# The causal mask inside the exponents' fp32r product, output rows kept earlier, routing weights later

## The reference, cut to what matters

```python
Lmat = jnp.exp(_segsum(Ac))          # exp(cs[l] - cs[s]) for s <= l, exp(-inf) = 0 above
Y_diag = jnp.einsum('bcln,bcsn,bhcls,bcshp->bclhp', Cc, Bc, Lmat, Xc)
Y_off = jnp.einsum('bcln,bchpn,bhcl->bclhp', Cc, states_prev, state_decay_out)
y = (Y_diag + Y_off + xs * D) * silu(z)
y = y * rsqrt(mean(y * y) + EPS) * rms_w ;  out = y @ W_out.T
weights, indices = top_k(softmax(xn @ router), 2);  norm_weights = softmax(weights)
return x + mamba(xn) + sum_k norm_weights_k * expert_k(xn)
```

## Time and profile before

| | |
|---|---|
| median of 3 runs | 715.56 us (715.31 to 716.43) |
| the profiled execution, its own time | 717.08 us |
| its span, first to last instruction | 715.1 us |
| busy share PE, DVE, ACT, POOL | 85%, 79%, 66%, 57% |
| mean granted TensorE clock | 0.952 |

### The profile page before, as it was taken

The page is one execution under the profiler, slowest core; times in us unless marked ns, Lnnn a source line. Parts: engine busy times, 40 slices in busy tenths (PEclk is TensorE's granted clock), DMA queues, the critical chain, the costliest instruction groups (busy, mean ns, idle before and its releaser), DMA issues. The chain is left out here.

```text
span 715.1 us, 15214 instructions
## 1 busy us (share of the span) xinstructions
PE 607.5 (85%) x3741; PEld 502.7 (70%) x3743; DVE 566.4 (79%) x1460; ACT 470.6 (66%) x1050; POOL 406.4 (57%) x606
## 2 busy tenths in 40 slices
PE   0879698999999999999999998699999999999600
PEld 0766376777777777777777777588888888888500
DVE  7799899989889898988989898666666666666264
ACT  3695667777787778887787875456666666666300
POOL 4000076777676776767777767326666666666700
PEclk9998999999999999999999999699999999999955
DMA  9980100000000000000000016233333333332189
GB/s 306 275 200 0 32 26 20 29 26 25 25 24 28 24 25 28 24 25 24 25 28 24 28 32 194 71 95 111 101 105 111 107 107 104 113 101 75 38 318 386
DMA packets 64940, 61.49 MB, mean 86 GB/s; under 512 B 9082, under 2 KB 56062, under 8 KB 64912
## 3 DMA queue, kind: packets, MB, share of 16 engines
q1 hardware_dynamic: 56464, 44.11, 21.5%
q0 software_dynamic: 8448, 17.06, 6.9%
HBM read 30.19 MB, written 31.47 MB: 86 GB/s over the span
## 5 line engine op out<-in xcount | busy, mean ns | idle before, releaser
L506 POOL DMA_INDIRECT moe_d<-raw,slot_st x136 | 133.7, 983 | 92.9 <-issue 71.4
L479 POOL DMA_INDIRECT slots_d<-rows,slot_st x128 | 140.6, 1099 | 73.8 <-POOL rows L474 52.5
L1197 DVE SCALAR_TENSOR_TENSOR act<-raw,taps,act 128x512 f32<-128x512 f32 x180 | 139.7, 776 | 13.4 <-ACT act L631 11.1
L785 ACT ACTIVATE l_sb<-bank 128x256 f32<-128x256 f32 x136 | 44.8, 381 | 74.0 <-PE bank L1057 74.0
L455 POOL TENSOR_TENSOR xde<-xb,e_end 128x256 f32<-128x256 f32 x64 | 44.9, 702 | 85.2 <-DVE xb L1384 83.9
L1499 DVE CAST x_hi<-bank 128x256 fp32r<-128x256 f32 x68 | 28.9, 424 | 64.7 <-PE bank L1066 64.7
L921 PE MATMUL bank<-xb,m_sb 128*128 128x64 f32 x512 | 69.3, 279 | 7.9 <-DVE y_sb L1404 3.9
L921 PEld LDWEIGHTS bank<-xb,m_sb 128*128 128x128 f32 x512 | 64.0, 194 | 16.3 <-DVE y_sb L1404 10.0
L1085 PE MATMUL bank<-act,raw 128*128 x544 | 72.0, 276 | 0.0
L1085 PEld LDWEIGHTS bank<-act,raw 128*128 128x128 f32 x544 | 66.1, 192 | 0.2 <-issue 0.2
L1057 PE MATMUL bank<-xw_hi,x_hi 128*128 x136 | 60.6, 446 | 5.5 <-DVE m_sb L1510 5.5
(11 more groups left out here) (244 smaller groups left out, 1641.5 us busy)
## 6 DMA issues: line engine op xcount, KB each, us to landing
slots_d<-rows SPq DMA_DIRECT2D x8, 1122.0 KB, 12.8
rows<-slots_d SPq DMA_DIRECT2D x68, 132.0 KB
x_sb<-in_x SPq DMA_DIRECT2D x8, 512.0 KB, 6.3
act<-in_x SPq DMA_DIRECT2D x64, 64.0 KB
xw_hi<-moe_d SPq DMA_DIRECT2D x8, 512.0 KB, 9.3
xw_lo<-moe_d SPq DMA_DIRECT2D x8, 512.0 KB, 10.0
out<-x_sb SPq DMA_DIRECT2D x8, 512.0 KB, 13.2
moe_d<-raw,slot_st POOLq DMA_INDIRECT x136, 2.3
```

Of the source, the lines that this page charges most:

```text
L479: nc.gpsimd.indirect_dma_start(out=slots_d, out_offset=bass.IndirectOffsetOnAxis(ap=slot_st[:, r, c:c + 1], axis=0), in_=rows[:, r, c, :], ...
L506: nc.gpsimd.indirect_dma_start(out=moe_d, out_offset=bass.IndirectOffsetOnAxis(ap=slot_st[:, r, c:c + 1], axis=0), in_=ym[r % R][:, c * D: ...
L785: a = A(l_sb[:, r % 2, c * F:(c + 1) * F], bank[2 + 2 * (r % 2) + c][:, 0:F], ACT.Silu)
L1197: V.scalar_tensor_tensor(out=group_act(par)[:, t, :], in0=proj[:, t, k:k + GT], scalar=taps[:, t, k:k + 1], in1=group_act(par)[:, t, :], o ...
```

## The change

The mask's product is gone. `dd_l` and `dd_r` have 128 rows instead of 10. Rows 0 to 9 are as before; rows 10 to 63 of `dd_r` are zero; rows 64 to 127 of `dd_r` are a 64x64 identity repeated along l, and the same rows of `dd_l` hold -1e30 for the 64 values of l in half f. Thus one product of 64 columns for each head gives difference and mask. There are two products for each tile, one for each half f of l, of 256 columns each, which read and write with gaps. POOL builds these rows once, behind its other preparation. The transfer of `ncs_d` into `dd_l` is made twice for each pair of tiles, once for each half.

`keep_out` copies only the 128 output columns; the sums of squares of a sequence's eight tiles go to eight columns of bank 7 and are copied once, at the sequence's last tile. At q = 2 `keep_out(nn - 3)` stands ahead of `tap0` and `decays`. Before the loop the slots are signalled before the two weights are worked out; the weights (`pair_weights`) come after the first `by_token`, and POOL alone waits for them (`pairs_done`). ACT takes the exponential for them ahead of the first `decays`.

```diff
-        dd_l = sb("dd_l", [10, 2, 2, P], F32R)
-        dd_r = sb("dd_r", [10, 2, 2 * NH * P], F32R)
+        dd_l = sb("dd_l", [P, 2, 2, 2, P], F32R)
+        dd_r = sb("dd_r", [P, 2, 2 * NH * P], F32R)
...
-                    sp.dma_start(dd_l[0:8, i % 2, :, :].bitcast(F32), ncs_d[:, bass.ds(n, 2), :])\
-                        .then_inc(ld_dd[i % 2], 16)
+                    for f in range(2):
+                        sp.dma_start(dd_l[0:8, i % 2, f, :, :].bitcast(F32), ncs_d[:, bass.ds(n, 2), :])\
+                            .then_inc(ld_dd[i % 2], 16)
...
+            behind = yo_sb[:, 0:192]
+            chain(pool.memset(behind, 0.0))
+            chain(pool.affine_select(out=behind, in_=behind, compare_op=ALU.is_ge, fill=MASKED, base=0,
+                                     pattern=[[-1, 192]], channel_multiplier=1))
+            for f in range(2):
+                rows_of = behind[:, 64 * (1 - f):64 * (1 - f) + P].unsqueeze(1).broadcast_to([P, 2, P])
+                for i in range(2):
+                    chain(pool.tensor_copy(dd_l[:, i, f, :, :], rows_of))
+            pool.memset(dd_l[0:64, :, :, :, :].bitcast(F32), 1.0).then_inc(mask_done, 1)
+            units = dd_r[64:P, :, :].rearrange("k i (b l) -> k (i b) l", l=64)
+            pool.tensor_copy(units, ident[64:P, 64:P].unsqueeze(1).broadcast_to([64, 8 * NH, 64])).then_inc(mask_done, 1)
...
             silu_first()
+            act_e.wait_ge(dp_done, 1)
+            A(tv[7], tv[6], ACT.Exp).then_inc(dp_exp, 1)
             decays(0, 0)
             halo(1, 1, 0)
             keep_proj(NAT, 0, 1)
-            act_e.wait_ge(dp_done, 1)
-            A(tv[7], tv[6], ACT.Exp).then_inc(dp_exp, 1)
...
-                A(x_sb[:, tile_ix(nn), :].rearrange("p a d -> p (a d)"), bank[7][:, 0:D], ACT.Copy)
-                A(ssq[:, tile_ix(nn)], bank[7][:, D:D + 1], ACT.Copy).then_inc(o_kept, 1)
+                o = A(x_sb[:, tile_ix(nn), :].rearrange("p a d -> p (a d)"), bank[7][:, 0:D], ACT.Copy)
+                if c == SC - 1:
+                    o = A(ssq[:, bass.ds(nn - c, SC)], bank[7][:, D:D + SC], ACT.Copy)
+                o.then_inc(o_kept, 1)
...
                             keep_proj(g6 + NAT, 0, g)
+                        if not (first and j < 4):
+                            keep_out(nn - 3, (j - 3) % SC)
+                        if not last:
                             act_e.wait_ge(front_done, nn + 2)
                             tap0(g6 + NAT, 0, g)
                         if more:
                             act_e.wait_ge(m_done, nn + 1)
                             decays(nn + 2, j % 2)
-                        if not (first and j < 4):
-                            keep_out(nn - 3)
...
-                mm(bank[2][:, :], dd_l[:, pr, o, :], dd_r[:, pr, o * NH * P:(o + 1) * NH * P], start=True, stop=False)
-                mm(bank[2][:, :], ident_b[:, :], mask_b[:, :].unsqueeze(1).broadcast_to([P, NH, P]),
-                   start=False, stop=True).then_inc(dd_done, 1)
+                halves = lambda t: t.rearrange("p (h f l) -> p h f l", h=NH, f=2)
+                for f in range(2):
+                    m = mm(halves(bank[2][:, :])[:, :, f, :], dd_l[:, pr, f, o, :],
+                           halves(dd_r[:, pr, o * NH * P:(o + 1) * NH * P])[:, :, f, :], start=True, stop=True)
+                m.then_inc(dd_done, 1)
...
-            dve.wait_ge(dp_exp, 1)
-            chain(V.tensor_scalar(tv[8], tv[7], 1.0, None, ALU.add))
-            chain(V.reciprocal(meta[:, :, 0, 1], tv[8]))
-            V.tensor_tensor(meta[:, :, 1, 1], tv[7], meta[:, :, 0, 1], ALU.mult).then_inc(slots_done, 1)
+            dve.sem_inc(slots_done, 1)
...
             by_token(0, 0, lambda: None)
+            pair_weights()
             other_taps(1, 1, 0, HALO)
```

More of the change, by code:

```diff
@@ L412, in _ @@
             pool.tensor_copy(rows[:, 0, 0, D:D + 1], tokid[:, 0:1]).then_inc(consts, 1)
-            for t, v in ((ident, 0.0), (upper, 1.0), (later_b, 0.0), (mask_b, 0.0)):
+            for t, v in ((ident, 0.0), (upper, 1.0), (later_b, 0.0)):
                 chain(pool.memset(t[:, :], v))
@@ L460, in prepare_ids @@
                 nn, r = b * SC + j, j % R
+                pool.wait_ge(pairs_done, 1)
                 if not (is_first(b) and j < R):
-                    pool.wait_ge(slots_done, 1)
                     pool.wait_ge(scat[r], 16 * K * (b * 2 + j // R))
@@ L534, in _ @@
                 for a in range(2):
-                    A(dd_r[0:8, i, a * NH * P:(a + 1) * NH * P], ddr0[0:8, :], ACT.Copy).then_inc(ddr_done, 1)
+                    A(dd_r[0:64, i, a * NH * P:(a + 1) * NH * P], ddr0[0:64, :], ACT.Copy).then_inc(ddr_done, 1)
             act_e.wait_ge(consts, 2)
@@ L706, in row, with keep_out @@
                   bias=nmr1[:, t], scale=r1[:, t]).then_inc(xn_done, 1)
-            def keep_out(nn):
+            def keep_out(nn, c):
                 act_e.wait_ge(norm_done, 4)
@@ L725, in sequence @@
                     if q < 3 and not (first and j < 4):
-                        keep_out(nn - 4)
+                        keep_out(nn - 4, (j - 4) % SC)
                     if q < 3:
@@ L772, in _ @@
             weights_high(3)
-            keep_out(NT - 4)
-            keep_out(NT - 3)
+            keep_out(NT - 4, SC - 4)
+            keep_out(NT - 3, SC - 3)
             for n_ in (NT - 2, NT - 1):
@@ L777, in _ @@
             for n_ in (NT - 2, NT - 1):
-                keep_out(n_)
+                keep_out(n_, n_ % SC)
             act_e.wait_ge(ms_done, 1)
@@ L933, in turn_y, with project_out @@
                 tp.then_inc(yt_done, 1)
-            def project_out(nn, u, early):
+            def project_out(nn, col, early):
+                u = col % 2
                 pe.wait_ge(sq_done, nn + 1)
@@ L941, in project_out @@
                 for c in range(2):
-                    m = mm(bank[7][:, D:D + 1], sq[:, u, c * P:(c + 1) * P], ones[:, 0:1], start=(c == 0),
+                    m = mm(bank[7][:, D + col:D + col + 1], sq[:, u, c * P:(c + 1) * P], ones[:, 0:1], start=(c == 0),
                            stop=(c == 1))
@@ L1004, in sequence @@
                     if not (first and j < 3):
-                        project_out(nn - 3, (j - 3) % 2, first and j < 4)
+                        project_out(nn - 3, (j - 3) % SC, first and j < 4)
                     if q == 3 and not (last and g == 1):
@@ L1023, in _ @@
             over_sequences(pe, sequence)
-            project_out(NT - 3, (NT - 3) % 2, False)
+            project_out(NT - 3, SC - 3, False)
             turn_y(NT - 1, (NT - 1) % 2, False)
-            project_out(NT - 2, (NT - 2) % 2, False)
-            project_out(NT - 1, (NT - 1) % 2, False)
+            project_out(NT - 2, SC - 2, False)
+            project_out(NT - 1, SC - 1, False)
             pe.wait_ge(o_kept, NT)
@@ L1103, in _ @@
                 V.memset(t[:, :].rearrange("p (b s) -> p b s", b=NB)[:, :, 0:PADW].bitcast(F32), 0.0)
-            V.memset(dd_l[:, :, :, :].bitcast(F32), 1.0)
             V.memset(dt6[:, :, NH:NH + 2], 1.0)
```

18 lines of the change are left out of this document (11 added, 7 removed).

## The result

The changed kernel took 718.78 us (median of 20, 716.54 to 720.27), the kernel before 716.11 us beside it (20 runs, 713.48 to 717.78): 1.0037 times as long, 95% interval 1.0027 to 1.0047. It is slower by 2.7 us where 709.4 was forecast, outside the range and on the side that had a chance of 0.05. The profiled execution took 719.17 us with a span of 717.1, 2.0 more than the span before.

A forecast was written before the change was run, and what follows sets the result against it. It took a ring through PE, ACT and DVE to bound the loop. From the median 715.56 us, -4.2 (loop), -2.2 (entry) and +0.2 (POOL's rows) made 709.4, range 707.5 to 711, for 8 in 10 703.5 to 713.

The forecast's parts named there:

- 14 x 0.3 = 4.2 us: Tile loop: keep_out ahead of tap0 without the one-column copy saves about 0.3 us in each of groups 1 to 14.
- the rule: POOL shares SBUF interfaces with VectorE and contends with its two-SBUF-input instructions; DVE's gate takes 424 ns, at worst 1070.
- GpSimd's rows: Preparation: building the mask rows on POOL disturbs DVE's first eight scalings, costing 0.2 us, between 0 and 5.2.
- the entry: Before the loop: slots signalled ahead of the pair weights let the first tiles start earlier, saving 2.2 us, bounds 1.2 and 3.3.
- its own bounds for the terms: Gains of 2.5 to 6.7 us for the loop and 1.2 to 3.3 us for the entry.
- The first taps: Entry to the loop: DVE's taps were to start at about 87.8 instead of 89.00, 1.2 us earlier.
- rival (d): Preparation: POOL holds DVE's first eight scalings, all behind is 5.2 us late, giving 714.4 us; chance 0.07.
- My bound of 0.65 an instruction: Preparation: the most that POOL could lengthen each of DVE's eight scalings, 8 x 0.65 = 5.2 us in all.
- The halves: Each tile: two 256-column products replace product and mask, freeing 0.23 to 0.33 us of PE; saving costed at nothing.
- Rival (e): Loop: a half is dear at 0.65 us, the pair takes 1.30, PE becomes the bound, 736 us; chance 0.05.
- my 0.34: Each tile: expected PE time in us for the pair of halves, bounds 0.23 and 1.30.
- The expert stage: Sign named in the prediction: the expert stage behind the loop stays unchanged in length.

The follow-up runs named there:

- e3: The kernel before with the early copy of the output at q = 2 and the eight ssq columns alone: 716.03 us, ratio 1.0000.
- e1: The changed kernel with the mask as it was; the early copies and late pair weights stay: 717.02 us, ratio 1.0013.
- e12: The changed kernel with the old mask, the ten products of e8 and the GpSimd copy of e9: 710.44 us, ratio 0.9931.
- e14: The kernel of e12 with more such TensorE products at three places behind the loop (4, 3 and 12): 710.87 us, ratio 0.9919.
- e10: The kernel before with one extra, unused GpSimd copy per tile in the six looped sequences: 714.78 us, ratio 0.9975.
- e13: The kernel before with the ten products of e8 at the same place: 713.48 us, ratio 0.9968.
- e2: The kernel before with the new mask alone, in two halves, its rows built in the preparation: 717.01 us, ratio 1.0015.
- e4: The changed kernel with GpSimd's building of the mask rows held back until the first half of the norm is done: 716.66 us, ratio 1.0009.
- e9: The changed kernel with one extra, unused GpSimd copy per tile in the six looped sequences: 714.72 us, ratio 0.9985.
- e8: The changed kernel with ten TensorE products into a free bank ahead of the middle product of tile 62: 715.63 us, ratio 0.9998.
- e5: The changed kernel with one more, unused GpSimd copy of 128x128 in each of the 64 tiles, ahead of the row copy: 719.79 us, ratio 1.0058.
- e6: The changed kernel with ScalarE writing both copies of a tile's rows and GpSimd none: 726.97 us, ratio 1.0154.
- e7: The kernel before with ScalarE writing both copies of a tile's rows and GpSimd none: 723.76 us, ratio 1.0110.

## Why the prediction was wrong

The step that failed is "14 x 0.3 = 4.2 us". It summed the path of VectorE out of instructions of fixed length and had no term for VectorE and GpSimd meeting in the loop. The path itself came out as forecast: TensorE's wait for the one-column copy went, VectorE's wait at q = 3 shrank from 0.91 to 0.46 us in the group of the earlier trace rows (to 0.33 by forecast), and the group won 0.28 us. But the fillers have two SBUF inputs, and wherever VectorE comes earlier it can meet GpSimd: 0.8 us of lead at j = 2 became 0.0 at j = 3, by one more hold of 0.62 in each sequence. In the loop the term measures 0 (45.48 us for eight tiles in before, e3 and after), and e3's time is the kernel before's. The prediction had the rule at hand, from the same gate of 1070 ns, and used it for the preparation only.

Of the 8.9 us between forecast and result (6.2 gained, 2.7 lost) the loop's term makes 4.2, GpSimd's rows 1.8 and the entry, if it came to nothing, 2.2. The stated range was too narrow besides: with its own bounds for the terms it would run from 705.8 to 712.1, and even that doesn't hold the result.

**The entry**, -2.2. The late pair weights do bring the entry forward. Gate 0 came at 98.1, 98.5 and 99.5 us in the three traces with the old mask and late weights (e1, e12, e14), and at 99.5, 99.8 and 99.9 in those with neither (e10, e3, e13): about 1 us, with the two sets touching. Counted from the last slots it is clearer, 14.4 to 15.0 us against 16.2 to 16.6; the wait for tap0, 1.2 to 1.6 us in e3, e10 and e13, is gone. The first taps are not earlier, as I had them: they come 2.63 us behind the last slots in e1, 2.76 in e3. In the trace of before, against which I worked, the weights waited 2.14 us for their exponential and 0.45 to 0.49 in the other three, and its gate 0 at 102.25 was itself some 2.4 us late (the clock of 60 to 70 us was 0.72 there and 1.00 in e3); a sum made against one execution took that over. Then the gain goes: from gate 1 to gate 2 it takes 8.85 us in before, e3, e10 and e13 and 10.48 after. There the gate of tile 1 takes 0.94 us instead of 0.46, a filler 1.23 instead of 0.74, and the seven small products of 136 columns 3.25 instead of 2.75, each beside GpSimd. e2 (halves alone) has the 10.49 as well, and e1, e12 and e14, which are one and the same program up to there, have 10.50, 8.84 and 11.11. So it belongs to the phase between the two engines and to no single edit. The late weights have no run of their own; by e1 less e3 they measure +0.13%, with intervals of 0.15% on each, where -2.2 us (-0.3%) was forecast.

**GpSimd's new rows**, +0.2 with an upper bound of 5.2. This is rival (d), a term mis-sized more than a mechanism missed: it measures 2.0 us (e4 against the changed kernel), where e4 hides the hold and doesn't remove it. In place it differs from what I wrote. Not the eight scalings were held, but one product of 32 columns ahead of them, for the length of the cast, 1.87 of 1.89 us. My bound of 0.65 an instruction came from a GpSimd instruction of 0.6 us; the hold is as long as the one that GpSimd happens to run.

**The halves.** Costed at nothing, and that is what they are in the loop (e2: 45.48 us for eight tiles). Rival (e), by which I went for "slower", has no part in it, so that the chance of 0.05 for "slower" stood on the wrong mechanism: the pair takes 277.04 - 276.81 = 0.23 us of TensorE where product and mask took 0.66, the lower bound and not my 0.34 (a q = 1, as there):

```profile
276.81 0.40 PE L911 MATMUL bank<-dd_r,dd_l 128*128 128x256 f32 x2
277.04 0.39 PE L920 MATMUL bank<-act 128*128 128x128 f32 x2
```

**The end of the loop** the prediction left out. The lead of 0.98 us at tile 57 is gone at tile 58 (432.80 against 432.68), where no fillers are left and GpSimd's xde is what TensorE waits for. From gate 56 to 63 it takes 31.7 us before and 35.2 after, 34.5 in e3, 32.4 in e2: in these traces the early copies lose 2 to 3 us there. Yet e3 is no slower than the kernel before in its median; single executions vary here, and how much of this stretch is the change's and how much the clock's stays open, since the fill gains in both kernels.

The expert stage kept its length, as forecast: from the last gate to the end of the span 260.3 us before and 259.7 after.

The sum by runs: e2 +0.15%, e3 0, e1 +0.13%, the whole +0.37%. The first and the third make 0.28%, which their intervals allow; the late pair weights are in e1 and have no run of their own.

## What to carry to other kernels

Where VectorE's instructions with two SBUF inputs and GpSimd's share a loop, a path sum needs a term for their meeting: look at min, median and max of such a line first, and expect that moving either engine by half a microsecond changes who stands. Try a delay of GpSimd before believing that the gained time is gone: here a useless copy was worth 4.1 us to the changed kernel and 1.8 to the one before, but the collision can move to the next instruction, as in e9. And where such a repair helps, give it to the kernel before as well.

Build constants on GpSimd beside a stretch in which VectorE waits anyway, and count each hold at the length of GpSimd's instruction, not of VectorE's. And take a start time from several executions, not one: the last slots varied by 1.4 us and gate 0 by 2.8 in four traces with the same instructions up to there (before, e3, e10, e13).

## What was not expected of the hardware

More work made the kernel faster: 48 GpSimd copies that nobody reads took 4.1 us from the changed kernel and 1.8 from the one before (e9, e10), and ten TensorE products of 2.55 us in all took 2.8 and 2.3 (e8, e13). One such copy in all 64 tiles took 0.76 us from each eight tiles of the loop, though not from the whole (e5). And with less work on GpSimd and more on ScalarE (e6, e7) the same fillers were 84 and 104 ns longer in the mean at the same median of 752.
